# First head pair's first pass inside the last projection chunk; first layer norm of the feed-forward part inside attention's last steps

## The reference, cut to what matters

```python
x = x + tanh(g_x) * xattn(ctx, layernorm(x), mask, mask)
x = x + tanh(g_f) * ffn(layernorm(x))

def xattn(src, tgt, src_mask, tgt_mask):
    k, v = split((src @ W_src.T + b_src) * src_mask)       # 512 each
    q = (tgt @ W_tgt.T + b_tgt) * tgt_mask
    scores = q @ k.T / 8, masked keys at -inf
    update = softmax(scores) @ v
    return concat(tgt, update) @ W_out.T + b_out

def ffn(x):                                                # 512 -> 2048 -> 512
    h = bit_linear(x, w1)       # tokens rounded to 8-bit integers by their maximum, weights ternary
    h = silu(depthwise_conv1d(h))                          # three taps along the tokens
    return bit_linear(h, w2)
```

## Time and profile before

| | us |
|---|---|
| median of 3 runs (1926.18 to 1927.2) | 1926.86 |
| the profiled execution | 1929.86 |
| its span (first to last instruction) | 1928.0 |
| PE busy | 1684.4 |
| DVE busy | 1216.9 |
| ACT busy | 780.3 |
| POOL busy | 729.0 |

### The profile page before, as it was taken

How to read it: one execution, slowest core, us unless ns; L and a number is a source line. 1 busy time by engine, 2 the same in 40 slices (tenths; PEclk the granted TensorE clock), 3 DMA queues, 4 the chain that set the end, 5 groups by cost and what they waited for, 6 DMA issues and landing times.

```text
span 1928.0 us, 24398 instructions
## 1 busy us (share of the span) xinstructions
PE 1684.4 (87%) x8738; PEld 1038.8 (54%) x8738; DVE 1216.9 (63%) x2270; ACT 780.3 (40%) x793; POOL 729.0 (38%) x317
## 2 busy tenths in 40 slices
PE   6887899999997699999999999999856785967867
PEld 5666678888885344455445444544433443534434
DVE  6777645343433567755765676465269979799793
ACT  2111122222210044433442344245318766787676
POOL 1121000000000088866885688578606134062340
PEclk9989999999998599999999999999979798997988
DMA  6656547444444511114111412041130030120201
GB/s 233 229 181 206 179 170 243 154 149 152 171 145 152 180 56 56 56 66 143 56 57 66 143 57 100 12 143 35 44 131 1 1 131 0 38 92 0 88 1 44
DMA packets 104676, 200.59 MB, mean 104 GB/s; under 512 B 7568, under 2 KB 27024, under 8 KB 104592
## 3 DMA queue, kind: packets, MB, share of 16 engines
q1 hardware_dynamic: 104592, 199.49, 29.5%
HBM read 127.90 MB, written 71.57 MB: 103 GB/s over the span
## 4 chain that ended last, share of the span: by engine, by line
PE 62%; issue 19%; POOL 7%; DVE 6%; DMA 5%; SPq 1%; ACT 1%; POOLq 0%; DVEq 0%; ACTq 0%
PE ps L1260 13%; PE ps L1272 12%; PE ps L1224 9%; PE ps L1226 9%; PE ps L1225 9%; PE ps L1244 6%; DMA wraw<-in_w2T 5%; POOL h_first L672 4%; POOL h_third L672 2%; PE ps L1285 2%; DVE junk L926 1%; PE ps L1461 1%; DVE h_first L1179 1%; POOL acc L667 1%; DVE gp L1158 1%
## 5 line engine op out<-in xcount | busy, mean ns | idle before, releaser
L667 POOL TENSOR_TENSOR acc<-acc,pr 128x1024 f32<-128x1024 f32 x192 | 457.7, 2384 | 118.7 <-ACT pr L684 99.6
L684 ACT ACTIVATE pr<-ps,mcol 128x1024 f32<-128x1024 f32 x256 | 284.3, 1114 | 405.1 <-PE ps L1260 402.3
L926 DVE CUSTOM_DVE_ANT_0 junk<-ps,mbias 128x512 bf16<-128x512 f32 x512 | 333.4, 689 | 171.8 <-PE ps L1244 168.0
L1272 PE MATMUL ps<-pr,vv 128*64 128x512 f32 x1024 | 273.3, 616 | 0.0
L672 POOL TENSOR_TENSOR h_first<-h_first,last_tap 128x1024 f32<-128x1024 f32 x44 | 104.8, 2385 | 306.2 <-ACT last_tap L804 306.2
L650 POOL MEMSET nmt<- 128x128 f32 x1 | 0.2, 204 | 449.1 <-DMA w_ternary<-wtb 449.1
L1244 PE MATMUL ps<-kh,qh 64*128 64x512 f32 x512 | 136.8, 475 | 26.3 <-DVE nmv L926 17.6
L1244 PEld LDWEIGHTS ps<-kh,qh 64*128 64x128 f32 x512 | 57.5, 193 | 148.3 <-issue 101.7
L1419 PE MATMUL ps<-xiT,w1q 128*128 128x512 bf16 x512 | 125.1, 393 | 5.9 <-ACT xiT L790 5.9
L1461 PE MATMUL ps<-w2q,hq 128*128 128x512 bf16 x512 | 120.8, 390 | 2.5 <-ACT hq L840 1.8
L667 POOL TENSOR_TENSOR acc<-pr 128x1024 f32<-128x1024 f32 x32 | 76.8, 2399 | 110.8 <-ACT pr L684 110.8
(11 more groups left out here) (152 smaller groups left out, 3179.7 us busy)
## 6 DMA issues: line engine op xcount, KB each, us to landing
craw<-in_ctxT SPq DMA_DIRECT2D x8, 2048.0 KB, 9.7
xa<-in_x SPq DMA_DIRECT2D x8, 1024.0 KB, 6.4
wraw<-in_w1T SPq DMA_DIRECT2D x16, 512.0 KB, 7.3
wraw<-in_w2T SPq DMA_DIRECT2D x16, 512.0 KB, 7.6
q_split<-kqh SPq DMA_DIRECT2D x32, 256.0 KB, 2.0
q_split<-kql SPq DMA_DIRECT2D x32, 256.0 KB, 2.3
base<-lna SPq DMA_DIRECT2D x8, 1024.0 KB, 9.1
k_split<-kqh SPq DMA_DIRECT2D x32, 256.0 KB, 2.2
```

What stands on the lines that cost most here:

```text
L667: nc.gpsimd.tensor_tensor(acc[:, blk % 2, :], first, pr[:, (8 * blk + j) % NP, :], ALU.add).then_inc(pool_acc, 1)
L684: act.activation(pr[:, u % NP, :], ps[:, 2 * (u % 2):2 * (u % 2) + 2, :].rearrange("p a t -> p (a t)"), ACT.Exp, bias=mcol[:, (u // 64) * ...
L926: dve.tensor_tensor_reduce(out=junk[:, e, :], in0=ps[:, 4 + e, :], in1=mbias[:, b % 2, kk * CH:(kk + 1) * CH], scale=-1.0, scalar=3.0e38, ...
L1272: last = pe.matmul(ps[64 * e:64 * e + 64, 6 + blk % 2, :], vv[:, g % 2, j, 64 * e:64 * e + 64], pr[:, u % NP, e * CH:(e + 1) * CH], start= ...
```

## The change

Three things.

1. The last chunk of stage B is written out (`last_chunk`). All 22 lead units stand inside it: in each key group `m` one ahead of step `k` = 3, one ahead of `k` = 6 and one behind the group, so 12; ten more in the value groups 0 (three), 1 (one), 2 (three) and 3 (three). The `rows` of group 0 follow value group 1. Units 0 to 11 alternate between banks 4, 5 and 6, 7, units 12 to 21 between 0, 1 and 2, 3. The loads that they need (mask row, second pair, mask columns, low parts, values) stand on SP right behind `load_qk(0)`, ahead of the chunk's own stores; `max_out(0)` and `max_rows(0)` stand between the value stores. ACT waits for the chunk's last stores before its first exponential.
2. The first layer norm of D stands in attention's steps: its eight DVE parts in s = 123 to 130, each ahead of `sums` and `finish`; the square root on ACT behind the first exponential of s = 126; `ln_row` on PE in s = 130, the turns in s = 131 and 132. The load of `xn` is issued at the start of group 15.
3. The last batch's projections alternate between banks 5 and 0.

Buffers are placed anew for it: `vv`, `ql`, `kl`, `maug` are two tensors each, and slot 0 of them lies where chunk 6 had its context.

```diff
@@ stage C, order tables
+        def first_bank(n):
+            return 4 if n >= LEAD else 4 + 2 * (n % 2) if n < 12 else 2 * (n % 2)
+        K_UNITS = {(m, part): 3 * m + part for m in range(PAIRS) for part in range(3)}
+        V_UNITS = {(0, 0): 12, (0, 1): 13, (0, 2): 14, (1, 0): 15, (2, 0): 16, (2, 1): 17, (2, 2): 18, (3, 0): 19, (3, 1): 20, (3, 2): 21}
+        def y_bank(b, i):
+            return 0 if b == B - 1 and i % 2 else 5
+        LN_STEPS = {123: (0,), 124: (1,), 125: (2,), 126: (3,), 127: (4,), 128: (5,), 129: (6,), 130: (7,)}
...
@@ SP
             load_qk(0)
+            sp.wait_ge(pe_bv, (NCH - 1) * CT + 8)
+            load_mrow(0)
             load_qk(1)
+            sp.dma_start(mcol[:], mask_cols).then_inc(sp_mcol, 16)
+            load_lo(0)
...
+            load_vv(0)
             b_chunk(B - 1, 1, True)
...
-            load_mrow(0)
-            sp.dma_start(mcol[:], mask_cols).then_inc(sp_mcol, 16)
-            load_lo(0)
-            load_vv(0)
...
@@ ACT
             act.wait_ge(dve_mbias, 2)
+            act.wait_ge(dve_b, NCH * B_DVE_N)
+            for sl in range(2):
+                act.wait_ge(sp_k_out[sl], 32 + 64 * NCH)
+            act.wait_ge(sp_wq_out, 16 + 32 * NCH)
...
+                    if a == 0 and s == 126:
+                        act_ln_std(act, 0)
+            act_ln_row(act, 0)
+            for u in range(NT // 2):
+                act_ln_turned(act, 0, u)
...
@@ DVE, attention
                 if s in TURNS:
-                    rows(TURNS[s])
+                    dve_rows(dve, TURNS[s])
+                for step in LN_STEPS.get(s, ()):
+                    if step == 5:
+                        dve.wait_ge(pe_pv, 16 * (NG - 1))
+                    steps[step]()
                 if s in ZBLK:
                     sums(ZBLK[s])
...
@@ DVE, last chunk
+                dve_bias(dve, 0)
+                dve.wait_ge(sp_mcol, 16)
...
+                for m in range(PAIRS):
+                    dve_tops(dve, K_UNITS[m, 0])
+                    dve_tops(dve, K_UNITS[m, 1])
+                    dve.wait_ge(pe_bk, (NCH - 1) * PAIRS + m + 1)
...
+                    dve_tops(dve, K_UNITS[m, 2])
...
@@ PE, last chunk
+                    def between(k):
+                        if k in (3, 6):
+                            pe_tops(pe, K_UNITS[m, k // 3 - 1])
+                    split_mm(pe, ps[:, m, :], ..., KS, between).then_inc(pe_bk, 1)
+                    pe_tops(pe, K_UNITS[m, 2])
...
+        def pe_tops(pe, n):
+            g, i, kk = n // 16, n % 16 // 2, n % 2
+            if n % 16 == 0:
+                pe.wait_ge(sp_qk[g % 3], 32 * (g // 3 + 1))
...
+            if 2 <= n < LEAD:
+                pe.wait_ge(dve_free4, use4["t", 0] + 1 if n == 16 else use4["a", n - 2] + 1)
+                pe.wait_ge(dve_free5, use5["b", n - 2] + 1)
...
@@ PE, attention
+                if s == 130:
+                    ln_row(pe, 0)
+                if s == 131:
+                    ln_turn(pe, 0, 0)
+                    ln_turn(pe, 0, 1)
                 for b, i in YS.get(s, ()):
                     project(b, i)
+                if s == 132:
+                    ln_turn(pe, 0, 2)
+                    ln_turn(pe, 0, 3)
```

More of the change, by code:

```diff
@@ L529, in b_chunk @@
                     sp.dma_start(vd[ds(c * CH + j * P, P), :], vst[:, j % 2, :]).then_inc(sp_v_out[j % 2], 16)
+                    if last and half and j == 1:
+                        max_out(0)
+                    if last and half and j == 2:
+                        max_rows(0)
                 sp.wait_ge(dve_b, c * B_DVE_N + B_DVE["wb1"])
@@ L599, in _ @@
                     load_mrow(b + 1)
+                if g == NG - 1:
+                    load_xn(0)
                 if g % PAIRS == 1 and b:
@@ L974, in finish @@
                 dve.wait_ge(pe_y, b * NT + i + 1)
[L975 removed]
+                dve.scalar_tensor_tensor(out=bx[:, i, :], in0=ps[:, y_bank(b, i), :], scalar=gate_x, in1=bx[:, i, :],
                                          op0=ALU.mult, op1=ALU.add).then_inc(dve_free5, 1)
[L978 to L986 removed]
+            steps = ln_steps(dve, 0)
             for s in range(MACROS):
@@ L1234, in ln_row, with ln_turn @@
             last.then_inc(pe_row, 1)
-        def c_pe(pe):
-            def tops(n):
-                g, i, kk = n // 16, n % 16 // 2, n % 2
-                if n % 16 == 0:
-                    pe.wait_ge(sp_qk[g % 3], 32 * (g // 3 + 1))
-                for e, free, use in heads(n):
-                    if use:
-                        pe.wait_ge(free, use)
-                    last = pe.matmul(ps[:, 4 + e, :], qh[g % 3][64 * e:64 * e + 64, i * P:(i + 1) * P],
-                                     kh[g % 3][64 * e:64 * e + 64, kk * CH:(kk + 1) * CH], start=True, stop=True)
-                last.then_inc(pe_mx, 1)
+        def ln_turn(pe, b, u):
+            pe.wait_ge(dve_ln, b * LN_DVE_N + LN_DVE[f"xi{2 * u + 1}"])
+            if u < 2:
+                pe.wait_ge(act_ln, b * LN_ACT_N + LN_ACT["row"])
+            else:
+                pe.wait_ge(act_ln, b * LN_ACT_N + LN_ACT[f"xT{u - 2}"])
+            for j in range(2):
+                for k in range(KD):
+                    last = pe.transpose(ps[:, 2 + u % 2, :].bitcast(BF16)[:, (j * KD + k) * P:(j * KD + k + 1) * P],
+                                        xi[:, 2 * u + j, k * P:(k + 1) * P], identb[:])
+            last.then_inc(pe_xt, 1)
@@ new lines, in pe_tops @@
+        def pe_tops(pe, n):
+            g, i, kk = n // 16, n % 16 // 2, n % 2
+            if n % 16 == 0:
+                pe.wait_ge(sp_qk[g % 3], 32 * (g // 3 + 1))
+            if n < 2:
+                pe.wait_ge(dve_b, (NCH - 2) * B_DVE_N + B_DVE[f"v{2 * n + 1}"])
+            elif n in (12, 13):
+                pe.wait_ge(dve_b, (NCH - 1) * B_DVE_N + B_DVE[f"k{2 * n - 23}"])
+            if 2 <= n < LEAD:
+                pe.wait_ge(dve_free4, use4["t", 0] + 1 if n == 16 else use4["a", n - 2] + 1)
+                pe.wait_ge(dve_free5, use5["b", n - 2] + 1)
+            for e, free, use in heads(n):
+                if n >= LEAD:
+                    pe.wait_ge(free, use)
+                last = pe.matmul(ps[:, first_bank(n) + e, :], qh[g % 3][64 * e:64 * e + 64, i * P:(i + 1) * P],
+                                 kh[g % 3][64 * e:64 * e + 64, kk * CH:(kk + 1) * CH], start=True, stop=True)
+            last.then_inc(pe_mx, 1)
```

298 lines of the change are left out of this document (163 added, 135 removed).

## The result

The changed kernel takes 1885.45 us (median of 4 runs, 1883.47 to 1887.4) against 1927.03 for the kernel before (4 runs): a ratio of 0.978, 95% interval 0.977 to 0.980, 41.6 us less. 1881 was forecast, with a range of 1867 to 1892. The profiled execution took 1887.4 (span 1885.6).

The account below looks back on a forecast made before the run. TensorE carries most of the chain but stands nearly idle at the lead units and before the last feed-forward. Gains of 33.0 at the front and 13.0 at the tail, 46.0 us, take the median from 1926.86 to 1881, range 1867 to 1892.

Parts of the forecast that it names:

- The stall at unit 0: Last chunk: TensorE stalls 9.5 us at the first lead unit, until its keys land at 578.7.
- The mask columns: Last chunk: queued behind other loads, they land at 584.4; VectorE's first reduction waits, costing unit 2 0.8 us more.
- The units in the chunk: Last chunk: each lead unit costs 0.45 us with the tile-shape change back, 8.1 us for 18; bounds 0.23 and 0.80.
- First exponential: Attention's start: waits for the ternary store (5.3 us) and table load (1.3) behind the last value group, so 639.0.
- The late keys: Attention's sixth macro step: third pair's keys land near 659.5, needed at 660.8; no cost, 3 us if the queue is slower.
- The tail: From attention's last steps to the first feed-forward matmul: layer norm moved under attention gains 13.0 us, that matmul at 1426.5.
- The turns: Layer norm beside GpSimd: each normalizing operation waits for one addition and each addition for one, 0.5 us between; chance 0.58.
- POOL additions of 2.85: Sign of the turns beside the layer norm: GpSimd's additions lengthened to 2.85 us.
- VectorE keeping the port: Rival, layer norm: VectorE holds the port for all eight operations; gain 21.5 us instead of 13, median 1872.4; chance 0.27.
- The undisturbed one: Rival, layer norm: no disturbance by GpSimd; feed-forward begins at 1412.7, gain 26.9 us, median 1866.9; chance 0.08.
- Slow units: Rival, last chunk: units wait for VectorE, 2.2 us each instead of 0.45, 31 us more, median 1912; chance 0.05.
- Clock down: Rival, last chunk: the stall drops TensorE to 1.2 GHz and it stays there, 40 us lost, median 1937; chance 0.02.

Follow-up runs that it names:

- experiment 2: Changed kernel with the first two pairs' keys, queries and mask columns issued one chunk earlier, the mask row ahead of the last value store: 1873.88 us.
- experiment 6: Changed kernel with the first two lead units of each projection group side by side behind 18 of its 24 matmuls: 1886.2 us.
- Experiment 7: Changed kernel with the second half of the ternary rounding and its store earlier, and the exponential's table loaded ahead of ScalarE's wait: 1884.49 us.
- experiment 3: Changed kernel with GpSimd's seven additions of attention's last block (31) cut from 1024 to 16 columns: 1875.08 us.
- six kernels with an equal front: The changed kernel, its repeat and four variants that change nothing in the front; their fronts spread from 1070.2 to 1072.4 us.
- front only: Changed kernel with only the lead units in the last chunk; layer norm behind attention and all projections in bank 5, as before: 1899.87 us.
- experiment 4: Changed kernel with normalizing moved behind block 30's ul, maxima, scales and integers later, TensorE's scales and turns behind later projections: 1875.87 us.
- experiment 8: The kernel of experiment 7 with the third pair's loads and next mask row ahead of batch 0's base, ternary weights only with pair group 2: 1881.54 us.

## Why the prediction was right, step by step

- **The stall at unit 0** (9.5 us) was 9.29. The lower clock behind it was charged with 2.3 and cost 2.8: from unit 0 to unit 2, with 15 projection matmuls between, 7.58 us passed (576.86 to 584.44), and 4.75 in experiment 2, where nothing stalls (568.39 to 573.14). Experiment 2 removes the two, 12.1 us, and gains 12.2 in the front.
- **The mask columns**, estimated at 584.4 in the time of before, landed at 581.4, 1.2 us earlier counted from the chunk's start. Unit 2 did not wait; experiment 6 shows how near it is.
- **The units in the chunk: the term that was mis-sized.** I took 0.45 (bounds 0.23 and 0.80); it is 0.64. I had added 0.11 at each of two places to the 0.23. The rows show three: the unit comes 0.09 later than in a run, the matmul behind it 0.20 and the next 0.11. 18 units make 3.4 us. The last value group ended 69.6 us after the chunk's start and not 65.3, 4.3 later. That the cost belongs to the change and not to the unit, the paired units show (6.99). The Trainium skill (TensorEngine Tiling (Array Packing), Key Properties) says that a change of tiling mode drains the engine, without a figure; the trace agrees in so far as 0.41 of the 0.64 us come with the way there and back. That they are a drain, no row shows.
- **First exponential** 6.6 us behind the last value group: 6.65, released as foreseen by the ternary store.
- **What I had left out:** attention's first two steps, 9.63 instead of 7.74. I had ScalarE waiting and left out what TensorE would do: idle for 3.23 us before the second step, it started it at the lower level (starts 0.43 apart until 646). With these 1.9 us and the 4.3 of the chunk, 33.0 forecast for the front became 26.8.
- **The late keys** were forecast 1.3 us ahead of their use. In the changed kernel they are issued at 655.01 and need 8.8 us, and the first unit that reads them stands at 665.17: 1.4 us to spare, at no cost. Experiment 7 pulls attention forward and the stall comes out.
- **The tail.** Counted back by the shift of 28.6 us (`uh` of block 29 at 1331.48 and 1360.08), normalizing began at 1369.9 (forecast 1369.8) and was over at 1383.1 (1385.4); `ul` of block 30 at 1388.4 (1390.9), TensorE's new idle 11.6 (15), first feed-forward matmul 1425.0 (1426.5). The square root's two table loads took 1.28 us each (1339.43 and 1341.04), and the next function followed 0.02 us later, as taken in the sum.
- **The turns** were right in form, one operation for each addition, and wrong in size. I had each side wait for the other, 0.5 us a turn, and "POOL additions of 2.85" among the signs. They did not come: the additions took 2.34 to 2.38. The 2.85 in the trace before belong to an addition that began behind VectorE's operation; here the first five of VectorE's operations each began behind an addition, so only VectorE waited. The Trainium skill (SBUF — State Buffer, Who interferes with whom) has the lock held for the whole instruction by whichever comes first. The trace agrees: 2.6 us for an operation of 0.53 that comes second, and 2.85 for an addition of 2.38 that does.
- **The sum.** 46.0 forecast, 41.6 measured: 33.0 against 26.8, 13.0 against 14.5, and 1.8 us of luck ahead of the change in the profiled run (42.4 of span). So the total is closer than its larger part: of the 6.2 us that the front fell short, the tail's 1.5 and these 1.8 cover about half.
- **The rivals.** VectorE keeping the port would have ended the step in 5.7 us; it took 13.2. The undisturbed one would be 3.75, which experiment 3 shows where GpSimd's additions are all but gone. Slow units: the seven groups with 18 units took 50.4 us, not 78. Clock down: the granted clock was 1.00 from 584.6 to 635.

What stays open is why the clock is back sooner in some executions of the same chunk. Where the 2.2 us of spread in the front lie, the rows do show. In four of the six kernels with an equal front, unit 1 still runs at the lower clock (0.79 at 581.72 in the changed one), and from unit 0 to unit 2 it takes 7.35 to 7.58 us. In the other two (front only, experiment 4) unit 1 is at full speed, the same way takes 6.26 and 6.21, and the front is 1070.2 instead of 1071.7 to 1072.4. In experiment 4 another 0.9 us lie in attention's first two steps (8.69 us). The 0.7 us given back behind the tail are open too.

## What to carry to other kernels

When work is moved into a stage that keeps an engine busy, look first at what its operands wait for: 12 us of the moved part's cost came from loads issued 4.7 us into the chunk for a matmul that stands 2.0 us into it, and their issue could simply be moved up. An operation that will wait for GpSimd's belongs behind what a third engine needs next; the same contention cost 9.45 us in front of `ul` and at most 2 behind it. And when a start is pulled forward, the next transfer in the queue sets the new start: shift both, or measure a gain that is taken back a few steps later.

## What the runs showed of the hardware

- Against back-to-back additions of 128x1024 on GpSimd, VectorE's one-tensor operations of 128x512 get through one for each addition, starts 2.5 us apart (2.56 to 2.60 us each instead of 0.53). From the second on each begins 0.06 to 0.07 us behind an addition, and the additions keep their 2.34 to 2.38 us. Where an operation of VectorE's began 0.07 us ahead of an addition, it was the addition that took longer (2.85).
- A pair of 64-row matmuls between 128-row ones costs 0.64 us at the full clock, a second pair beside the first about 0.24 (6.99 us for a group where one pair joins another, 7.39 where none does).
- A SyncE queue that has issued three loads of 2 MB holds the next issue for 13.0 us (641.94; 12.94 in experiment 7), and what stands behind it in the queue comes later by that much. Where they stand behind it, the same issue took 0.33 us (638.69 in experiment 8).
- The switch to the exponential's table is 1.28 us and can be taken ahead of a wait by an exponential of one column (635.62).
